# A transformer block with experts on one core: the kept rows and residuals of seven sequences get homes of their own and are loaded during the first group's blocks, the eighth's stay in SBUF

## The chip, the core and the metric

The kernel runs on one core of a Trainium2 chip. The metric is the time of one execution on the device in microseconds (us); lower is better. TensorE (PE) multiplies, VectorE (DVE), ScalarE (ACT) and GpSimd (POOL) do the elementwise work, SyncE (SP) issues most of the DMA transfers, POOL the indirect ones. Each engine, SP too, works through its own list of instructions in order, and waits on semaphores.

## The reference

Eight sequences of 512 tokens of width 256, all in fp32. `_L0_attn_ref` is causal attention with 16 heads and rotary positions; `_L0_ffn_ref` routes every token to 4 of 16 experts and adds a shared expert:

```python
x = L0_attn_x
x = x + _layernorm(_L0_attn_ref(_layernorm(x, axis=-1), ...), axis=-1)
x = x + _layernorm(_L0_ffn_ref(_layernorm(x, axis=-1), ...), axis=-1)
# inside _L0_ffn_ref, with cw the gates of the 4 chosen experts:
y = jnp.einsum('nei,ne,ehi->nh', act, cw, Wd)
shared = silu(xf @ Ws_g.T) * (xf @ Ws_u.T) @ Ws_d.T
return x + y + shared
```

So the last step of a sequence needs, per token, the four expert rows, the sum `z` of the shared expert's output and the normed input, and the residual `x1` from after the attention. `z` and `x1` (512 KB each for a sequence) are made early, in the attention part, and used at the very end. They are the "kept rows and residuals", and together the kept pair of a sequence (1 MB).

## The kernel before

**Stages.** The attention part runs over the sequences 0 to 7; at its end each sequence's normed rows are scattered by POOL into `sorted_rows` in DRAM, in the order of their experts. The sequences form two groups, 0 to 4 and 5 to 7 (`GROUPS`). The block part then takes the sorted rows 128 at a time. Two blocks are a pair: 48 pairs for group 0 and 32 for group 1, 80 in all (numbers 0 to 79 below). For each pair SP loads the rows (`BLD`, `load_block`, tile `xg`, four pairs of buffers), PE transposes (`BT1`, L1522), multiplies by gate and up weights (`BGU`, L1536), transposes (`BT2`, L1549) and multiplies down (`BDN`, L1557). In one iteration PE does `BT1` of pair j, `BGU` of j-1, `BT2` of j-2 and `BDN` of j-3. ACT copies the result of `BDN` into `ys` (three buffers), and POOL scatters it to `expert_rows` in DRAM. DVE's `block_notes` (L1038 to L1048) reads a pair's notes; it gives the places for the scatter and lets SP load the pair four further on.

**The end of a sequence.** When all pairs of a group are scattered, its sequences are summed in halves of 256 tokens. `CZ` (`load_residuals`, L637 and L638) loads a kept pair from DRAM into `zt` and `x1t`; `CL` (`load_sums`, L650) loads a half's expert rows, 1 MB, into `ykt`; `CA` sums them with `z`, `CS` takes statistics, `CN` makes the rows and stores them (`store_out`, L655). Group 0's sums run on DVE, beside group 1's blocks; group 1's run after all blocks, with PE doing the sums over experts (L1436). `ykt`, `zt` and `x1t` have two homes, by the parity of the sequence; sequence 7 has its own (`*_last`). So a kept pair can be loaded only when the sequence two before it has been stored.

**Order.** `make_plan` gives each step a time, sorts all steps, and every engine walks the same list. `sums(g)` lists the side steps of a group. Group 0's 45 steps are spread evenly over group 1's iterations 5 to 30; group 1's come after the last pair. The last sequence's work between attention and scatter is stretched (`late`) over the first 25 or so pairs of group 0. Also in SP's list: `PAD` (`pad_rows`, L610 and L611), 16 small writes of zeros for group 1's rows, between pairs 25 and 36, and `store_z`, `store_x1`, which write a sequence's `z` and `x1` tiles to DRAM. One DMA queue carries all of SP's transfers.

**Memory.** The block part lays `xg`, `ykt`, `zt`, `x1t` over the attention's tiles. The tiles `xr`, `pr`, `x1`, `z`, `a_hi`, `a_lo`, `silu`, `act` and `att` of the attention part are not used again once the last sequence is through.

Of the kernel before, what the change touches and what calls it, by code (L numbers as in the profile page):

```python
# [100 lines left out]
B_START = 3 * N_QUAD + 10  # L101


def sums(g):

    first, end = GROUPS[g]
    halves = [(s, h) for s in range(first, end) for h in range(2)]
    if end == B:

        steps = [("CZ", g, s) for s in range(first, end)] + [("CL", g, *half) for half in halves]  # L110
        for i, (s, h) in enumerate(halves):
            steps += [("CA", g, s, h), ("CS", g, s, h)]
            if i:
                steps.append(("CN", g, *halves[i - 1]))
        return steps + [("CN", g, *halves[-1])]
    steps = [("CZ", g, s) for s in range(first, min(first + 2, end))] + [("CL", g, *halves[0]), ("CL", g, *halves[1])]
    for i, (s, h) in enumerate(halves):
        if i + 2 < len(halves):
            steps.append(("CL", g, *halves[i + 2]))
        steps += [("CA", g, s, h), ("CS", g, s, h)]  # L120
        if i:
            steps.append(("CN", g, *halves[i - 1]))
        if h == 0 and first < s and s + 1 < end:
            steps.append(("CZ", g, s + 1))
# [14 lines left out]
def make_plan():  # L139
    timed = []  # L140

    def add(time, *step):
        timed.append((time, len(timed), step))

    per_seq = 3 * QUADS
    for s in range(B):
        for item in BEFORE + AFTER:
            add(per_seq * s + late(s, sooner(s, item[0], item[-1])) + FILL, item[0], s, *item[1:-1])
        for q in range(QUADS):
            add(per_seq * s + 3 * q - 4.7, "STL", QUADS * s + q)  # L150
    for g, (a, b) in enumerate(GROUPS):
        add(per_seq * (b - 1) + late(b - 1, 34.75) + FILL, "GE", g)
        add(per_seq * (b - 1) + late(b - 1, 38.1) + FILL, "GR", g)
        for e in range(E):
            add(per_seq * (b - 1) + late(b - 1, 35 + 0.42 * e) + FILL, "PAD", g, e)
        add(6 + 8 * g, "DUM", g)
    for Q in range(N_QUAD):
        for n in range(2 * UNITS):
            block, second = n // 2, n % 2
            add(3 * Q + block + (0.1, 0.3)[second], "S", Q, n // UNITS, n % UNITS)  # L160
            add(3 * Q + 7 + block + (0.0, 0.2)[second], "ST", Q, second, block)
        for m in range(UNITS):
# [12 lines left out]
    for g in range(len(GROUPS)):
        side = sums(g)
        begin = B_START + DUO0[g] + duos(g) + 5
        gap = (duos(g + 1) - 7) / len(side) if g + 1 < len(GROUPS) else 0.5
        for n, step in enumerate(side):
            add(begin + gap * n + 0.45, *step)  # L180
    return [step for _, _, step in sorted(timed)]
# [51 lines left out]
def block_kernel(nc, x, w_small, w_exp, rope, consts, out):  # L233
# [4 lines left out]
    with ctx:  # L238
# [42 lines left out]
        h_hi = place("h_hi", [P, KD, T], fp32r)  # L281
        h_lo = place("h_lo", [P, KD, T], fp32r)
        w_high = cursor[0]
        xr = place("xr", [P, 2, NT, XROW])
        pr = place("pr", [P, NT, D])
        x1 = place("x1", [P, NT, D])
        z = place("z", [P, NT, D])
        a_hi = place("a_hi", [P, 2, T], fp32r)
        a_lo = place("a_lo", [P, 2, T], fp32r)
        silu = place("silu", [P, 2, T])  # L290
        act = place("act", [P, 2, T])
        att = place("att", [P, NT, D])
        o_t = place("o_t", [P, T])
        mrow = place("mrow", [4 * NT, 2, P], fp32r)
# [76 lines left out]

        cursor[0] = w_low
        ykt_last = place("ykt_last", [P, NT, TOPK, D])
        zt_last = place("zt_last", [P, NT, D])
        x1t_last = place("x1t_last", [P, NT, D])
        assert cursor[0] <= w_high

        ident = kc[:, K_IDENT:K_IDENT + P]
        pcol = kc[:, K_PCOL:K_PCOL + 1]
# [100 lines left out]
        s_ys = sem("block_rows_out")  # L480
        s_ysc = [sem(f"block_scattered{i}") for i in range(NYS)]
        s_cl = [sem(f"parts_back{i}") for i in range(6)]
        s_cz = [sem(f"residuals_back{i}") for i in range(3)]
        s_cp = sem("results_summed")
        s_cs = sem("final_sums")
        s_cst = sem("final_stats")
        s_cv = sem("final_variance")
        s_cr = sem("final_rstd")
        s_cn = sem("final_rows")
        s_out = [sem(f"out_stored{i}") for i in range(3)]  # L490

        RELEASE = {
            "S": lambda st: (s_max, MAX_DONE[st[1:]]),
# [33 lines left out]

        def back(s):

            if s == B - 1:  # L530
                return ykt_last, zt_last, x1t_last
            return ykt[:, s % 2, :, :, :], zt[:, s % 2, :, :], x1t[:, s % 2, :, :]

        def sums_before(s, h):

# [8 lines left out]
        def _(sp):  # L544
# [85 lines left out]

            def load_residuals(s):
                _, z_home, x1_home = back(s)
                if turn(s) > 1:
                    sp.wait_ge(s_out[home(s)], 32 * (turn(s) - 1))
                sp.wait_ge(s_zst, 16 * (s + 1))
                sp.wait_ge(s_x1st, 16 * (s + 1))
                sp.dma_start(z_home[:, :, :], packed(z_dram[s])).then_inc(s_cz[home(s)], 16)  # L637
                sp.dma_start(x1_home[:, :, :], packed(x1_dram[s])).then_inc(s_cz[home(s)], 16)  # L638

            def load_sums(s, h):  # L640
                g = group_of(s)
# [10 lines left out]
            def store_out(s, h):  # L652
                sp.wait_ge(s_cn, N_OUT * (2 * s + h + 1))
                tiles = slice(NHALF * h, NHALF * h + NHALF)
                sp.dma_start(rows(out[s])[:, tiles, :], back(s)[1][:, tiles, :]).then_inc(s_out[home(s)], 16)  # L655

            load_x(0)
            sp.dma_start(stage[:, 0:C_O], w_small[:, 0:C_O]).then_inc(s_wq, 16)
# [4 lines left out]
            for st in PLAN:  # L663
# [8 lines left out]
                    maxima_rows(n)  # L672
                elif kind == "X1L":
                    load_x1(n)
                elif kind == "LNC":
                    store_x1(n)
                elif kind == "Z":
                    store_z(n)
                elif kind == "DUM":
                    zero_dummies(n)  # L680
# [4 lines left out]
                elif kind == "BLD":  # L685
                    load_block(n, st[2])
                elif kind == "CZ":
                    load_residuals(st[2])
                elif kind == "CL":
                    load_sums(st[2], st[3])  # L690
                elif kind == "CN":
                    store_out(st[2], st[3])
            for place_of in range(3):
                sp.wait_ge(s_out[place_of], 32 * max(turn(s) for s in range(B) if home(s) == place_of))


        @block.gpsimd
# [74 lines left out]
        def _(dve):  # L772
# [284 lines left out]
            def final_sums(s, h):  # L1057
# [1 line left out]
                y, z_home = back(s)[0][:, tiles, :, :], back(s)[1]  # L1059
                done = sums_before(s, h)  # L1060
                if s >= SHARED:
                    if h == 0:
                        dve.wait_ge(s_cz[home(s)], 32 * turn(s))
                    n = 2 * (s - SHARED) + h
                    dve.wait_ge(s_cp, n + 1)
                    total = ring[2][:, n % 2, :].rearrange("p (t d) -> p t d", t=NHALF)
# [3 lines left out]
                dve.tensor_tensor(y[:, :, 2, :], y[:, :, 2, :], y[:, :, 3, :], ALU.add).then_inc(s_cs, 1)  # L1070
                dve.tensor_tensor(y[:, :, 0, :], y[:, :, 0, :], y[:, :, 1, :], ALU.add).then_inc(s_cs, 1)
                if h == 0:
                    dve.wait_ge(s_cz[s % 2], 32 * (s // 2 + 1))
                dve.wait_ge(s_cs, done + 1)
                dve.tensor_tensor(y[:, :, 2, :], y[:, :, 2, :], zt[:, s % 2, tiles, :], ALU.add).then_inc(s_cs, 1)
                dve.wait_ge(s_cs, done + 3)
                dve.tensor_tensor(y[:, :, 0, :], y[:, :, 0, :], y[:, :, 2, :], ALU.add).then_inc(s_cs, 1)

# [561 lines left out]
```

## Time and profile before

| | |
|---|---|
| three runs | 980.75, 982.78, 987.75 us (median 982.78) |
| span of the profiled execution | 1048.8 us |
| PE busy | 852.6 us (81%) |
| VectorE busy | 652.3 us (62%) |
| ScalarE busy | 456.3 us (44%) |
| GpSimd busy | 426.7 us (41%) |
| DMA moved | 168.72 MB, mean 161 GB/s |
| SP's queue (q1) | 128.85 MB, 42.1% of 16 engines |
| POOL's queue (q0) | 38.55 MB, 9.9% |

Times in the trace count from the first instruction. A busy share is an average over stages with different limits: the attention part ends near 656 us, group 0's pairs leave from 674 to 885 us, group 1's from 888 to 1005 us, and the rest is the sums of sequences 5 to 7. The profiled execution is 66 us longer than the median of the runs, so a number of the trace is that of one, slower, execution.

### The profile page before, as it was taken

What the parts mean: (1) busy time and instruction counts of PE and PEld (TensorE: products, weight loads), DVE (VectorE), ACT (ScalarE), POOL (GpSimd) and SP (SyncE); (2) the same over time, 40 slices, a digit from 0 to 9 for tenths busy, and PEclk for the clock granted to TensorE, in tenths of its full rate; (3) what the DMA queues carried; (4) which work ended last, traced back from release to release, by engine and by line L of the source; (5) the groups of instructions that cost most, each with busy time, mean ns of one, the idle gap of its engine ahead of it and who ended that gap; (6) DMA issues with size and microseconds to landing.
All of it is one profiled execution on the core that took longest, in us unless ns stands there. A gap on an engine that the chain in (4) does not pass through costs nothing.

```text
span 1048.8 us, 20609 instructions
## 1 busy us (share of the span) xinstructions
PE 852.6 (81%) x6580; PEld 615.2 (59%) x6580; DVE 652.3 (62%) x1914; ACT 456.3 (44%) x763; POOL 426.7 (41%) x408
## 2 busy tenths in 40 slices
PE   4569798987987987987987877978977799989955
PEld 3436374664664663664654545757865588867722
DVE  5577658687687687687586674533642233687916
ACT  2115454544544544544543555425433355544410
POOL 3222113135335335335213234374565555664621
PEclk9759898997897897997987998889999999998978
DMA  4685726236336336336395212453545566997783
GB/s 161 147 222 144 216 64 163 75 98 174 98 99 173 99 99 173 98 81 172 98 322 159 85 47 92 144 167 93 166 150 161 161 178 164 383 314 281 247 339 128
DMA packets 89175, 168.72 MB, mean 161 GB/s; under 512 B 14704, under 2 KB 56688, under 8 KB 88816
## 3 DMA queue, kind: packets, MB, share of 16 engines
q1 hardware_dynamic: 75248, 128.85, 42.1%
q0 software_dynamic: 13824, 38.55, 9.9%
q8 instruction: 57, 0.93, 0.4%
q14 instruction: 46, 0.38, 0.1%
HBM read 90.15 MB, written 76.68 MB: 159 GB/s over the span
## 4 chain that ended last, share of the span: by engine, by line
PE 40%; DVE 23%; issue 11%; SPq 8%; DMA 6%; another core or an unknown queue 5%; ACT 4%; POOL 3%; DVEq 0%; ACTq 0%; POOLq 0%
DVE nmax L829 8%; PE ring L1536 6%; PE ring L1314 5%; PE ring L1316 4%; PE ring L1315 4%; PE ring L1392 3%; PE ring L1557 3%; PE ring L1358 2%; SPq L628 2%; PE ring L1383 2%; SPq L629 2%; DMA xg<-sorted_rows 2%; PE ring L1436 2%; PE ring L1522 2%
## 5 line engine op out<-in xcount | busy, mean ns | idle before, releaser
L1244 ACT ACTIVATE prob<-ring 128x1024 f32<-128x1024 f32 (+1 forms) x192 | 167.5, 881 | 215.5 <-PE ring L1383 196.5
L829 DVE TENSOR_REDUCE nmax<-ring 128x2 f32<-128x1024 f32 (+3 forms) x256 | 201.8, 819 | 73.3 <-PE ring L1365 43.6
L736 POOL DMA_INDIRECT expert_rows<-ys,dest x160 | 159.2, 995 | 127.0 <-ACT ys L1198 74.8
L728 POOL DMA_INDIRECT sorted_rows<-xr,idx_all x128 | 130.5, 1019 | 104.8 <-DVE xr L991 71.5
L1536 PE MATMUL ring<-we,xh 128*128 x640 | 160.3, 396 | 0.0
L1536 PEld LDWEIGHTS ring<-we,xh 128*128 128x128 f32 x640 | 121.6, 200 | 14.6
L1054 DVE SCALAR_TENSOR_TENSOR sl<-sl,got,ring 128x128 f32<-128x128 f32 x160 | 48.3, 343 | 109.8 <-ACT sl L1296 62.5
L1358 PE MATMUL ring<-k_st,q_st 48*128 48x512 f32 (+3 forms) x512 | 88.9, 387 | 26.0 <-issue 9.7
L1392 PE MATMUL ring<-prob,v_sb 128*32 128x512 f32 (+3 forms) x1024 | 106.3, 518 | 3.2 <-ACT prob L1244 3.2
L1377 PE MATMUL ring<-maskt_b,halves_b 64*128 64x128 bf16 (+2 forms) x768 | 58.4, 233 | 50.7 <-DVE nmax L829 23.5
L1377 PEld LDWEIGHTS ring<-maskt_b,halves_b 64*128 64x128 bf16 x768 | 22.8, 97 | 125.4 <-issue 56.7
L1383 PE MATMUL ring<-q_st,k_st 50*128 50x384 f32 (+3 forms) x512 | 94.1, 406 | 0.0
L1557 PE MATMUL ring<-we,ah 128*128 x320 | 86.4, 394 | 5.4 <-ACT ys L1198 4.1
L706 POOL TENSOR_TENSOR rot<-rot 128x512 f32<-128x512 f32 x14 | 17.9, 1276 | 172.7 <-DVE rot L810 172.7
L1522 PE MATMUL ring<-kc,xg 128*128 128x128 f32 x320 | 51.7, 286 | 28.2 <-DMA xg<-sorted_rows 22.3
L1358 PEld LDWEIGHTS ring<-k_st,q_st 48*128 48x128 f32 x512 | 51.7, 220 | 38.9 <-issue 11.8
L1296 ACT ACTIVATE sl<-ring 128x256 f32<-128x256 f32 x80 | 30.8, 385 | 92.4 <-PE ring L1536 56.9
L1198 ACT ACTIVATE ys<-ring 128x512 f32<-128x512 f32 x80 | 47.8, 598 | 43.6 <-PE ring L1557 20.3
L1198 ACT ACTIVATE xh<-ring 128x512 f32<-128x512 f32 x80 | 47.7, 596 | 40.6 <-PE ring L1522 23.9
L1522 PEld LDWEIGHTS ring<-kc,xg 128*128 128x128 f32 x320 | 40.5, 147 | 39.9 <-DMA xg<-sorted_rows 27.0
L1557 PEld LDWEIGHTS ring<-we,ah 128*128 128x128 f32 x320 | 56.3, 196 | 11.8 <-issue 6.9
L1365 PE MATMUL ring<-mask_b,halves_b 64*128 64x128 bf16 (+2 forms) x768 | 62.6, 247 | 0.0
(203 smaller groups left out, 1650.8 us busy)
## 6 DMA issues: line engine op xcount, KB each, us to landing
xg<-sorted_rows SPq DMA_DIRECT2D x160, 134.0 KB
parts<-part SPq DMA_DIRECT2D x32, 512.0 KB
ykt<-expert_rows SPq DMA_DIRECT2D x14, 1024.0 KB
k_st<-parts SPq DMA_DIRECT2D x64, 128.0 KB
q_st<-parts SPq DMA_DIRECT2D x64, 128.0 KB
we<-w_exp SPq DMA_DIRECT2D x1, 6144.0 KB
sorted_rows<-zeros SPq DMA_DIRECT2D x2, 2144.0 KB, 9.6
sorted_rows<-zeros SPq DMA_DIRECT2D x32, 134.0 KB
```

The costliest lines, as they stand in the source:

```text
L728: pool.indirect_dma_start(out=xs[group_of(s)], out_offset=bass.IndirectOffsetOnAxis(ap=idx_all[:, s, t, k:k + 1], axis=0), in_=xr[:, s % 2 ...
L736: pool.indirect_dma_start(out=yk, out_offset=bass.IndirectOffsetOnAxis(ap=dest[:, j % 8, b:b + 1], axis=0), in_=ys[:, j % NYS, b, :], in_o ...
L829: dve.tensor_reduce(nmax[:, Q % 2, :, pp, qb], slot[:, :, col:col + (qb + 1) * P], AX.X, ALU.max, negate=True).then_inc(s_max, 1)
L1198: act_e.activation(dst, src, ACT.Copy).then_inc(done, 1)
L1244: act_e.activation(prob[:, u % 2, 2 * half:2 * half + 2, 0:width], slot[:, :, 0:width], ACT.Exp, scale=SCALE).then_inc(s_exp, 1)
L1358: pe.matmul(slot[:, par, col:col + width], q_st[r, Q % NQ, pp, q0:q0 + P], k_st[r, Q % NQ, pp, 0:width], start=n == 0, stop=False, skip_gr ...
L1377: pe.matmul(blocks_of(slot[:, par, :], diagonal)[:, :, 0:64 * (h + 1)], halves_b[r, h, :], mask, start=h == 0, stop=False, skip_group_chec ...
L1383: last = pe.matmul(slot[:, par, col:col + width], k_st[r, Q % NQ, half, k0:k0 + P], q_st[r, Q % NQ, half, k0:T], start=False, stop=True, s ...
L1392: last = pe.matmul(O_BANK[32 * j:32 * j + 32, kb * P:T], v_sb[:, s % 2, kb, 4 * q + j, :], prob[:, u % 2, j, col:col + T - kb * P], start= ...
L1522: last = pe.transpose(X_BANK[:, b, k, :], xg[:, j % NXG, b, k * P:(k + 1) * P], ident)
L1536: last = pe.matmul(G_BANK[j % 2][:, b, :], xh[:, j % 2, b, k, :], we_cols[:, bass.ds(columns[j, b] + k * D, D)], start=(k == 0), stop=(k = ...
L1557: last = pe.matmul(Y_BANK[:, b, :], ah[:, j % 2, b, :], we_cols[:, bass.ds(columns.pop((j, b)) + KD * D, D)], start=True, stop=True)
```

## The change

- `sums` has no `CZ` steps any more. Seven `CZ` steps, in the order of sequences 0, 1, 2, 3, 5, 6, 4, stand at iterations 20, 23.5, ... 41 of group 0's blocks.
- Sequences 2 to 6 get homes of their own in the place of attention tiles that are dead by then: `kept_z2` to `kept_z6`, `kept_x2` to `kept_x6`. Sequences 0 and 1 keep `zt` and `x1t`. Sequence 7's pair isn't stored or loaded: the sums read the tiles `z` and `x1`.
- `load_residuals` waits for no output store now, but for all `z`, and for sequence 4 (whose home is `xr`) for all scatters of rows.
- The 40 side steps of group 0 are spread over the same iterations as the 45 before.

```diff
+KEPT_ORDER = [0, 1, 2, 3, 5, 6, 4]
+KEPT_START, KEPT_STEP = 20, 3.5
...
-        steps = [("CZ", g, s) for s in range(first, end)] + [("CL", g, *half) for half in halves]
+        steps = [("CL", g, *half) for half in halves]
...
-    steps = [("CZ", g, s) for s in range(first, min(first + 2, end))] + [("CL", g, *halves[0]), ("CL", g, *halves[1])]
+    steps = [("CL", g, *halves[0]), ("CL", g, *halves[1])]
...
-        if h == 0 and first < s and s + 1 < end:
-            steps.append(("CZ", g, s + 1))
...
+    for n, s in enumerate(KEPT_ORDER):
+        add(B_START + KEPT_START + KEPT_STEP * n + 0.45, "CZ", s)
...
-        zt_last = place("zt_last", [P, NT, D])
-        x1t_last = place("x1t_last", [P, NT, D])
+        kept_z6 = place("kept_z6", [P, NT, D])
+        kept_x6 = place("kept_x6", [P, NT, D])
         assert cursor[0] <= w_high
+
+
+        cursor[0] = xr_at
+        kept_z4 = place("kept_z4", [P, NT, D])
+        kept_x4 = place("kept_x4", [P, NT, D])
+        assert cursor[0] <= pr_at
+        kept_z5 = place("kept_z5", [P, NT, D], offset=pr_at)
+        kept_x5 = place("kept_x5", [P, NT, D], offset=att_at)
+        kept_z2 = place("kept_z2", [P, NT, D], offset=a_at)
+        kept_x2 = place("kept_x2", [P, NT, D], offset=a_at + NT * D * 4)
+        kept_z3 = place("kept_z3", [P, NT, D], offset=silu_at)
+        kept_x3 = place("kept_x3", [P, NT, D], offset=silu_at + NT * D * 4)
+        kept = [(zt[:, 0, :, :], x1t[:, 0, :, :]), (zt[:, 1, :, :], x1t[:, 1, :, :]), (kept_z2, kept_x2), (kept_z3, kept_x3),
+                (kept_z4, kept_x4), (kept_z5, kept_x5), (kept_z6, kept_x6), (z, x1)]
...
                 _, z_home, x1_home = back(s)
-                if turn(s) > 1:
-                    sp.wait_ge(s_out[home(s)], 32 * (turn(s) - 1))
                 sp.wait_ge(s_zst, 16 * (s + 1))
                 sp.wait_ge(s_x1st, 16 * (s + 1))
-                sp.dma_start(z_home[:, :, :], packed(z_dram[s])).then_inc(s_cz[home(s)], 16)
-                sp.dma_start(x1_home[:, :, :], packed(x1_dram[s])).then_inc(s_cz[home(s)], 16)
+                sp.wait_ge(s_z, NHALF * B)
+                if s == 4:
+                    for par in range(2):
+                        sp.wait_ge(s_sc[par], 256 * (B // 2))
+                sp.dma_start(z_home[:, :, :], packed(z_dram[s])).then_inc(s_cz[s], 16)
+                sp.dma_start(x1_home[:, :, :], packed(x1_dram[s])).then_inc(s_cz[s], 16)
...
-                elif kind == "LNC":
+                elif kind == "LNC" and n < B - 1:
                     store_x1(n)
-                elif kind == "Z":
+                elif kind == "Z" and n < B - 1:
                     store_z(n)
...
-                    if h == 0:
-                        dve.wait_ge(s_cz[home(s)], 32 * turn(s))
+                    if h == 0 and s < B - 1:
+                        dve.wait_ge(s_cz[s], 32)
...
-                dve.tensor_tensor(y[:, :, 2, :], y[:, :, 2, :], zt[:, s % 2, tiles, :], ALU.add).then_inc(s_cs, 1)
+                dve.tensor_tensor(y[:, :, 2, :], y[:, :, 2, :], z_home[:, tiles, :], ALU.add).then_inc(s_cs, 1)
```

How SP's list moves, at three places. First, SP in group 1, behind the `BLD` of pair 65 and ahead of that of pair 66, before:

```order
L629 DMA xg<-sorted_rows 128x268
L637 DMA zt<-z_rows 128x1024 [waits x1_stored,z_stored,out_stored0]
L638 DMA x1t<-x_rows 128x1024
L650 DMA ykt<-expert_rows 128x2x1024 [waits final_rows]
L628 TENSOR_LOAD tab [waits block_places,block_transposed]
```

and in the changed kernel at the load of the same expert rows (sequence 2, first half; L673 is the old L650, L649 and L650 the old L628 and L629):

```order
L678 DMA out<-zt 128x2x256 [waits final_rows]
L673 DMA ykt<-expert_rows 128x2x1024 [waits final_rows]
L649 TENSOR_LOAD tab [waits block_places,block_transposed]
L649 ISA x2
L650 ISA
L650 DMA xg<-sorted_rows 128x268
L649 TENSOR_LOAD tab
```

The two loads of the kept pair of sequence 2, with their wait for an output store, are gone from between `xg` and expert rows; an output store (L678) stands closer to them now. Second, SP beside the pads, before, at the ninth of the 16 pads (L610, L611) and the `BLD` of pair 31 behind it:

```order
L610 TENSOR_LOAD pad_idx [waits pad_places]
L610 ISA x2
L611 ISA
L611 DMA sorted_rows<-zeros 128x268
L628 TENSOR_LOAD tab [waits block_places,block_transposed]
L628 ISA x2
L629 ISA
L629 DMA xg<-sorted_rows 128x268
```

and in the changed kernel, at the same pad (L631, L632), with the kept pair of sequence 2 (`kept_z_151` is `kept_z2`, `kept_x_152` is `kept_x2`) between it and the `BLD`:

```order
L631 TENSOR_LOAD pad_idx [waits pad_places]
L631 ISA x2
L632 ISA
L632 DMA sorted_rows<-zeros 128x268
L660 DMA kept_z_151<-z_rows 128x1024 [waits z_ready,x1_stored,z_stored]
L661 DMA kept_x_152<-x_rows 128x1024
L649 TENSOR_LOAD tab [waits block_places,block_transposed]
L649 ISA x2
L650 ISA
L650 DMA xg<-sorted_rows 128x268
L649 TENSOR_LOAD tab
```

The rows are the same but for the two loads, which wait for all `z` and for the stores. Third, SP's end, before, from the last `xg` on:

```order
L629 DMA xg<-sorted_rows 128x268
L655 DMA out<-zt 128x2x256 [waits final_rows] x3
L637 DMA zt<-z_rows 128x1024 [waits x1_stored,z_stored,out_stored1]
L638 DMA x1t<-x_rows 128x1024
L637 DMA zt<-z_rows 128x1024 [waits x1_stored,z_stored,out_stored0]
L638 DMA x1t<-x_rows 128x1024
L637 DMA zt_last<-z_rows 128x1024 [waits x1_stored,z_stored]
L638 DMA x1t_last<-x_rows 128x1024
L650 DMA ykt<-expert_rows 128x2x1024 [waits block_scattered2,final_rows,block_scattered1,block_scattered0]
L650 DMA ykt<-expert_rows 128x2x1024 [waits final_rows] x3
L650 DMA ykt_last<-expert_rows 128x2x1024 x2
```

and in the changed kernel:

```order
L650 DMA xg<-sorted_rows 128x268
L678 DMA out<-kept_z_147 128x2x256 [waits final_rows] x2
L673 DMA ykt<-expert_rows 128x2x1024 [waits block_scattered2,final_rows,block_scattered1,block_scattered0]
L673 DMA ykt<-expert_rows 128x2x1024 [waits final_rows] x3
L673 DMA ykt_last<-expert_rows 128x2x1024 x2
```

The six loads between the last output stores of group 0 and the first expert rows of group 1 are gone.

## Rows read from the trace of the kernel before

**Rows 1.** Windows: engines' busy us, granted clock, DMA share, GB/s; last two stages

```profile
core 0 of [0], span 1048.8 us
...
757.00:840.00 83.00, 62.34 (x302) 49.87 (x301) 27.29 (x130) 29.83 (x68) 47.83 (x50) 0.94 0.50 158
...
888.00:1005.00 117.00, 103.33 (x530) 86.30 (x527) 83.46 (x291) 52.87 (x118) 70.51 (x73) 0.96 0.85 308
```

**Rows 2.** Timeline of ACT: `ys` copies of pairs 34, 54, 57, 62, 67, 72, 79

```profile
842.75 0.60 ACT L1198 ACTIVATE ys<-ring 128x512 f32<-128x512 f32 x1 [0.42 <-PE ring L1557]
...
907.75 0.60 ACT L1198 ACTIVATE ys<-ring 128x512 f32<-128x512 f32 x1 [0.43 <-issue]
...
920.21 0.60 ACT L1198 ACTIVATE ys<-ring 128x512 f32<-128x512 f32 x1 [0.52 <-PE ring L1557]
...
936.86 0.60 ACT L1198 ACTIVATE ys<-ring 128x512 f32<-128x512 f32 x1 [0.51 <-PE ring L1557]
...
960.90 0.60 ACT L1198 ACTIVATE ys<-ring 128x512 f32<-128x512 f32 x1 [0.81 <-issue]
...
980.99 0.60 ACT L1198 ACTIVATE ys<-ring 128x512 f32<-128x512 f32 x1 [0.42 <-issue]
...
1005.29 0.60 ACT L1198 ACTIVATE ys<-ring 128x512 f32<-128x512 f32 x1 [2.67 <-DMA expert_rows<-ys,dest]
```

**Rows 3.** Timeline of PE, group 1: start, us, and in brackets the wait before

```profile
941.04 1.12 PE L1522 MATMUL ring<-kc,xg 128*128 128x128 f32 x4 [4.22 <-DMA xg<-sorted_rows]
...
962.80 0.66 PE L1522 MATMUL ring<-kc,xg 128*128 128x128 f32 x4 [2.32 <-DMA xg<-sorted_rows]
...
983.00 0.66 PE L1522 MATMUL ring<-kc,xg 128*128 128x128 f32 x4 [2.05 <-DMA xg<-sorted_rows]
```

**Rows 4.** Chain of waits: start, us, what; loads from issue to landing

```profile
834.97 4.23 DMA xg<-sorted_rows
...
895.49 9.94 DMA ykt<-expert_rows
...
933.92 7.07 DMA xg<-sorted_rows
...
954.67 8.09 DMA xg<-sorted_rows
```

**Rows 5.** Timeline of SP's queue ahead of the first of the three waits

```profile
928.37 1.23 SPq L629 DMA_DIRECT2D xg<-sorted_rows  x2
929.90 0.20 SPq L637 DMA_DIRECT2D zt<-z_rows  x1
930.15 0.42 SPq L638 DMA_DIRECT2D x1t<-x_rows  x1
930.62 0.43 SPq L650 DMA_DIRECT2D ykt<-expert_rows  x1
```

**Rows 6.** DMA view of 892 to 1000 us: rate in 40 equal slices

```profile
GB/s 258 376 416 410 408 409 418 410 405 250 263 354 291 221 239 343 348 383 418 348 13 219 278 299 381 372 414 374 132 208 303 335 397 384 192 155 97 145 285 367
```

**Rows 7.** Tail: chain's scatters to landing, and POOL's next-to-last scatter in the timeline

```profile
995.42 6.52 DMA expert_rows<-ys,dest
...
1007.42 2.56 DMA expert_rows<-ys,dest
...
1006.16 0.96 POOL L736 DMA_INDIRECT expert_rows<-ys,dest  x1 [0.54 <-ACT ys L1198]
```

**Rows 8.** Pad stretch: chain on SP, SP's timeline after the pads, PE's waits 757 to 840

```profile
788.41 0.69 SPq L611
...
805.27 0.34 SPq L610
...
806.47 0.47 SPq L625
...
830.84 19.44 SPq L629 DMA_DIRECT2D xg<-sorted_rows  x15
...
PE ring L1522 <- DMA xg<-sorted_rows: 13.7, 8, 3.6
```

More of the change, by code:

```diff
@@ L283, in block_kernel @@
         w_high = cursor[0]
+        xr_at = cursor[0]
         xr = place("xr", [P, 2, NT, XROW])
+        pr_at = cursor[0]
         pr = place("pr", [P, NT, D])
@@ L287, in block_kernel @@
         z = place("z", [P, NT, D])
+        a_at = cursor[0]
         a_hi = place("a_hi", [P, 2, T], fp32r)
         a_lo = place("a_lo", [P, 2, T], fp32r)
+        silu_at = cursor[0]
         silu = place("silu", [P, 2, T])
         act = place("act", [P, 2, T])
+        att_at = cursor[0]
         att = place("att", [P, NT, D])
@@ L482, in block_kernel @@
         s_cl = [sem(f"parts_back{i}") for i in range(6)]
-        s_cz = [sem(f"residuals_back{i}") for i in range(3)]
+        s_cz = [sem(f"residuals_back{s}") for s in range(B - 1)]
         s_cp = sem("results_summed")
@@ L489, in block_kernel @@
         s_cn = sem("final_rows")
-        s_out = [sem(f"out_stored{i}") for i in range(3)]
+        s_out = sem("out_stored")
         RELEASE = {
@@ L528, in back @@
         def back(s):
-            if s == B - 1:
-                return ykt_last, zt_last, x1t_last
-            return ykt[:, s % 2, :, :, :], zt[:, s % 2, :, :], x1t[:, s % 2, :, :]
+            return ykt_last if s == B - 1 else ykt[:, s % 2, :, :, :], *kept[s]
         def sums_before(s, h):
@@ L654, in store_out @@
                 tiles = slice(NHALF * h, NHALF * h + NHALF)
-                sp.dma_start(rows(out[s])[:, tiles, :], back(s)[1][:, tiles, :]).then_inc(s_out[home(s)], 16)
+                sp.dma_start(rows(out[s])[:, tiles, :], back(s)[1][:, tiles, :]).then_inc(s_out, 16)
             load_x(0)
@@ L687, in _ @@
                 elif kind == "CZ":
-                    load_residuals(st[2])
+                    load_residuals(n)
                 elif kind == "CL":
@@ L692, in _ @@
                     store_out(st[2], st[3])
-            for place_of in range(3):
-                sp.wait_ge(s_out[place_of], 32 * max(turn(s) for s in range(B) if home(s) == place_of))
+            sp.wait_ge(s_out, 32 * B)
         @block.gpsimd
@@ L1072, in final_sums @@
                 if h == 0:
-                    dve.wait_ge(s_cz[s % 2], 32 * (s // 2 + 1))
+                    dve.wait_ge(s_cz[s], 32)
                 dve.wait_ge(s_cs, done + 1)
-                dve.tensor_tensor(y[:, :, 2, :], y[:, :, 2, :], zt[:, s % 2, tiles, :], ALU.add).then_inc(s_cs, 1)
+                dve.tensor_tensor(y[:, :, 2, :], y[:, :, 2, :], z_home[:, tiles, :], ALU.add).then_inc(s_cs, 1)
                 dve.wait_ge(s_cs, done + 3)
```

## The prediction

> **What bounds the kernel now.** I read the windows by stage first, then the times at which the blocks leave, then the chain of waits, and last the SP queue. The profiled execution spans 1048.8 us [rows 1], against a median of 982.78 us in the three runs. I make the sum in the profiled execution and carry its difference over to the median, and say below what the 66 us between them can do to it.
>
> The last of the four matmul steps of a pair of blocks ends in a `ys` copy. From pair 34 (842.75) to pair 54 (907.75) twenty pairs leave in 65.00 us [rows 2]: 3.25 us each, and PE is the bound there. From pair 54 to pair 79 (1005.29) 25 pairs take 97.54 us where 81.25 would do: 16.3 us are lost. This is the stretch in which group 0's sums run beside group 1's blocks, and the DMA engines are 0.85 busy in it, at 308 GB/s, against 0.50 and 158 in the stretch ahead [rows 1]. The 16.3 us split at the same rows: pairs 54 to 57 lose 12.46 - 9.75 = 2.71; 57 to 62 lose 16.65 - 16.25 = 0.40; 62 to 67 lose 24.04 - 16.25 = 7.79; 67 to 72 lose 20.09 - 16.25 = 3.84; 72 to 79 lose 24.30 - 22.75 = 1.55.
>
> The three large ones have one cause. PE waits for `xg` exactly three times, 4.22, 2.32 and 2.05 us [rows 3]. These transfers took 7.07 and 8.09 us to land (the first two are on the chain) where one in the quiet stretch took 4.23 [rows 4]. Ahead of each stands the same pattern on SP's queue, of which the first is shown: both tiles of a kept pair (`zt`, `x1t`, 1 MB), then 1 MB of expert rows, then the `xg` [rows 5]. The first loss, 54 to 57, has another form: the first load of expert rows stands behind two kept pairs (2 MB) and lands after 9.94 us [rows 4], and VectorE, which also makes the notes of each block, waits for it.
>
> **The change part by part.** (1) *Five kept pairs leave group 1's stretch* (5 MB). What one costs there: SP goes on from the end of the `xg` issue (928.37 + 1.23 = 929.60) to the issue of the expert rows (930.62), 1.02 us [rows 5]; and its bytes stand ahead of the `xg` in the queue. The DMA engines carry 408 to 418 GB/s when they are full [rows 6], so 1.05 MB takes 2.56 us. An `xg` behind it comes 3.6 us sooner. Against the waits of 2.32 and 2.05 that is enough, so 3.84 and 1.55 go; of 4.22 it leaves 0.6, and I keep 1.5 of the 7.79, for the gap and for a clock that may still dip: 6.3 saved. Of the 2.71 of the first burst I count half, 1.3: 2 MB fewer ahead of the first expert rows is 5.1 us, more than the wait, but VectorE still does two halves of sums between the notes of two pairs. Sum 13.0. Bounds: 16.3, if nothing is left; and 5.4 (3.84 + 1.55) if the first stall stays.
>
> The Trainium skill (DMA: Bandwidth & Descriptors, section "Where 436 GB/s comes from") puts the limit of HBM-to-SBUF traffic at about 358 GB/s for a core; the trace goes over that here. By the page's figure a kept pair would take 2.9 us, an estimate, and the first stall would shrink to about 0.3 us; the measured rate decides, and the sum stays.
>
> (2) *The tail.* Three kept pairs were issued while the last scatters ran; a scatter then took 6.52 us to land, and the last one, with the burst gone by, 2.56 [rows 7]. ACT's `ys` copies wait for those landings. But POOL has a backlog of scatters and sat idle only 0.54 us before its last two [rows 7], so no more than that comes off the end. I take 0.5 (bounds 0 and 2, if POOL starts its last run sooner). What follows, the loads of expert rows and PE's sums over them, reads nothing that the change touches.
>
> (3) *Spacing.* The 45 side steps of group 0 become 40 over the same 25 iterations, so a load has 1.9 iterations ahead of its sum (before 1.7). Nothing; the cover is VectorE's idle time.
>
> (4) *Two stores and a pair of loads of sequence 7 are gone.* The stores (1 MB) lie in group 0's stretch, which has half its DMA time free [rows 1]; nothing, at most the 1 us of two issues.
>
> (5) *Seven kept pairs enter group 0's blocks*, 14 DMAs on SP. None waits: all `z` were written before, the stores landed long ago, and the last scatters of rows are some ten iterations ahead of the pair of sequence 4, which alone needs them. Behind each stands a `BLD`, and PE waits for that. Three (sequences 5, 6, 4) fall where PE is full and SP stands up to four pairs ahead, 13 us, against 1.02 + 2.56: nothing. Four (0, 1, 2, 3) fall beside the 16 pad rows. There SP is itself near the bound: a pair's two `xg` take about 19.4 / 7.5 = 2.6 us, a pad 806.47 - 805.27 = 1.20 [rows 8]. Over the twelve pairs with 16 pads that is 12 x 2.6 + 16 x 1.2 = 50.4 us against PE's 39.0: 11.4 us over, and the lead of 13 us, less a landing of 4.23 [rows 4], covers 8.8. So before, some 2.6 us are already lost there and SP is the bound; what is added to SP counts in full. The pair of sequence 0 stands ahead of the pads, where SP has 3.25 - 2.6 = 0.65 us to spare with each pair and regains most of it; the other three stand among the pads, 3 x 1.02 = 3.1 us. The bytes add nothing lasting, as PE has room to catch up, but for the last: 2.56 at most. Take 3.0. Bounds: 0, if SP is quicker without the profiler, and 6.5.
>
> Sum: -13.0 - 0.5 + 3.0 = -10.5 us, so 1038.3 in this span's terms and 982.8 - 10.5 = 972.3 in the runs'.
>
> *The 66 us.* In this trace SP often advances one instruction in 0.7 us in the pad stretch (788.41, a register instruction, 0.69) [rows 8], and PE waits 13.7 us for `xg` there [rows 8]. Such steps are rare from 888 on, where the losses are tied to bytes. I hold the first for the profiler's own load, which the runs do not have, and the second for real. That is a choice, not something that the trace shows.
>
> **The rivals.** *A: as summed*, 972.3, own range 967 to 977. Chance 0.60. *B: more comes off*: nothing of 16.3 is left, POOL gains 2 and SP hides the moved loads: 982.8 - 18 = 965. For it: DMA demand falls from 0.85 x 117 = 99 us by 5 MB at 2.56, 13, to 86 us for 117 us. Chance 0.09. *C: the bursts of expert rows do the harm by themselves*: ten of 1 MB stay, each with an `xg` behind it, and the first stall (4.22) stays with its low clock; 5.4 + 0.5 - 3.0 = 2.9 comes off, 980. Against it: loads of expert rows without a kept pair ahead (two of three) made no wait of PE. Chance 0.22. *D: SP's queue becomes the bound, slower than before*: if the 0.7 us steps are real, a moved pair costs SP its five or so instructions at 0.7, 3.5 us, and a late `xg` 2.56 more; four of them 24 us, less 13.5: +10.7, 993.5. It decides from 3.4 us per moved pair on (4 x 3.4 = 13.6). For it: PE's 13.7 us of waits in this trace; against it: the runs are 66 us shorter than this trace, so they cannot hold all of it. Chance 0.09.
>
> That the change doesn't do what it says is no case: the order of SP's rows shows the loads gone from group 1.
>
> **How the numbers follow.** The range must leave out no more than 0.2: D (0.09) and a part of B and of C's far end; 964 to 982. One per cent is 9.8 us, to 972.95, and about what these runs (980.75 to 987.75) can tell from no change. A lies across that bound: 0.6 of it, 0.36, is faster, with B 0.45; the rest of A and C 0.46; D 0.09.
>
> **What would show it.** Right: no PE wait over 1 us for `xg` in group 1's pairs, pairs 54 to 79 in 84 us or so, DMA share there near 0.75, the first expert rows landing in 5 us, and the time from pair 20 to pair 34 longer by some 3 us. Wrong: a wait for `xg` behind expert rows alone (C), or SP late by more than 13 us in the pads, with PE waiting at each moved pair (D).

## The result, and the profile after

Over twenty runs each the changed kernel takes 978.94 us and the kernel before 985.43 us in the median: ratio 0.9941, 95% interval 0.9925 to 0.9958. A second comparison (label e13_after_again) gave 0.9944, 0.9921 to 0.9968. That is 5.8 us faster (4.1 to 7.4), where 10.5 was forecast. The sign is right, the size a bit over half.

The trace on record of the kernel before spans 66 us more than the runs take in the median, so two more were taken of it; they span 986.9 us (e0_before) and 984.8 us (e12_before_again). The second stands for the kernel before from here on. Its `ys` copies of pairs 20, 34, 54 and 79 (timeline of ACT; start, us, ..., wait before):

```profile
720.73 0.60 ACT L1198 ACTIVATE ys<-ring 128x512 f32<-128x512 f32 x1 [0.52 <-PE ring L1557]
...
775.10 0.60 ACT L1198 ACTIVATE ys<-ring 128x512 f32<-128x512 f32 x1 [0.57 <-PE ring L1557]
...
840.10 0.60 ACT L1198 ACTIVATE ys<-ring 128x512 f32<-128x512 f32 x1 [0.43 <-PE ring L1557]
...
941.27 0.60 ACT L1198 ACTIVATE ys<-ring 128x512 f32<-128x512 f32 x1 [3.04 <-DMA expert_rows<-ys,dest]
```

The same copies in the changed kernel, whose profiled execution spans 976.7 us:

```profile
720.59 0.60 ACT L1220 ACTIVATE ys<-ring 128x512 f32<-128x512 f32 x1 [0.51 <-PE ring L1579]
...
778.58 0.60 ACT L1220 ACTIVATE ys<-ring 128x512 f32<-128x512 f32 x1 [0.43 <-PE ring L1579]
...
843.58 0.60 ACT L1220 ACTIVATE ys<-ring 128x512 f32<-128x512 f32 x1 [0.43 <-PE ring L1579]
...
931.33 0.60 ACT L1220 ACTIVATE ys<-ring 128x512 f32<-128x512 f32 x1 [1.41 <-PE ring L1579]
```

Take 3.25 us per pair off each stretch, and what a stretch loses is left. (The last pairs, with fewer matmuls beside them, can leave less than 3.25 us apart, so a stretch that ends at pair 79 can lose less than nothing.) From the `ys` copies of each trace (us; the tail is from pair 79's copy to the end of the span):

| trace | pairs 20 to 34 | 34 to 54 | 54 to 79 | tail |
|---|---|---|---|---|
| before, on record | 25.7 | 0.0 | 16.3 | 43.5 |
| before, e0_before | 7.5 | 0.0 | 21.1 | 43.6 |
| before, e12_before_again | 8.9 | 0.0 | 19.9 | 43.5 |
| after | 12.5 | 0.0 | 6.5 | 45.4 |
| after, e13_after_again | 14.2 | 0.0 | 7.6 | 45.5 |

Between the means of the last two traces before and the two after: +5.2 us among the pads, -13.5 in group 1, +1.9 in the tail, together -6.4. That is the 5.8 us of the runs, within what they can tell. Two traces of a kernel differ by 1 to 2 us in a stretch, so the parts are no surer than that.

The cut at pair 79's copy divides things that belong together, and the 13.5 us have two halves. From pair 54 to 72 the loss went from 16.7 us to 10.0 (means of two traces each), from pair 72 to 79 from 3.9 to -2.9.

The three large waits of [rows 3] have these three in their place (timeline of PE after, group 1):

```profile
863.05 1.12 PE L1544 MATMUL ring<-kc,xg 128*128 128x128 f32 x4 [2.87 <-DMA xg<-sorted_rows]
...
888.70 0.66 PE L1544 MATMUL ring<-kc,xg 128*128 128x128 f32 x4 [1.28 <-DMA xg<-sorted_rows]
...
907.81 0.66 PE L1544 MATMUL ring<-kc,xg 128*128 128x128 f32 x4 [2.58 <-DMA xg<-sorted_rows]
```

and among the pads stand these three:

```profile
735.01 0.66 PE L1544 MATMUL ring<-kc,xg 128*128 128x128 f32 x4 [1.24 <-DMA xg<-sorted_rows]
...
748.79 0.66 PE L1544 MATMUL ring<-kc,xg 128*128 128x128 f32 x4 [3.70 <-DMA xg<-sorted_rows]
...
766.90 1.10 PE L1544 MATMUL ring<-kc,xg 128*128 128x128 f32 x4 [3.21 <-DMA xg<-sorted_rows]
```

Their sum and count against before (waits of PE, 720 to 780 us, e12_before_again and then after; us in total, times, longest):

```profile
PE ring L1522 <- DMA xg<-sorted_rows: 5.1, 5, 2.0
```

```profile
PE ring L1544 <- DMA xg<-sorted_rows: 8.1, 3, 3.7
```

So the waits themselves grew by 3.0 us and the stretch by 3.6 between these two traces. Between the other two, e0_before and e13_after_again, the waits went from 4.4 us to 8.7 and the stretch from 7.5 to 14.2. Behind a long wait PE is slow besides. The windows of the changed kernel behind two of the waits (from and to, length, busy us of PE, PEld, DVE, ACT and POOL, then granted clock, DMA share, GB/s) show a granted clock of 0.76:

```profile
749.00:756.00 7.00, 7.00 (x31) 5.83 (x30) 1.69 (x9) 2.45 (x5) 5.18 (x6) 0.76 0.76 242
767.00:774.00 7.00, 7.00 (x30) 5.98 (x31) 1.81 (x10) 2.34 (x5) 3.11 (x4) 0.76 0.75 232
```

One wait of 3.70 us made pair 28 leave 5.6 us late, one of 3.21 pair 32 by 5.1. So each cost 1.9 us more than its length. In the chain the eight matmuls behind the first took 2.87 us, against 1.73 at full clock:

```profile
743.92 4.82 DMA xg<-sorted_rows
748.75 0.04 issue
748.79 0.66 PE ring L1544 x4
749.45 2.87 PE ring L1558 x8
```

### The profile page after: what moved, and what is told of

Read it like the earlier page. It is cut to its first block, busy times and chain, and to the rows that moved or that the text cites. A ratio compares the mean times of both kernels' runs of the same rounds, so it can differ in the third digit from the quotient of the medians.

```text
span 976.7 us, 20603 instructions
## 1 busy us (share of the span) xinstructions
PE 819.3 (84%) x6580; PEld 601.5 (62%) x6580; DVE 651.2 (67%) x1914; ACT 453.5 (46%) x763; POOL 426.7 (44%) x408
## 4 chain that ended last, share of the span: by engine, by line
PE 49%; DVE 23%; issue 7%; DMA 6%; ACT 5%; SPq 5%; POOL 4%; DVEq 0%; ACTq 0%; POOLq 0%
PE ring L1558 10%; DVE nmax L851 7%; PE ring L1336 5%; PE ring L1338 4%; PE ring L1337 4%; PE ring L1579 4%; PE ring L1414 3%; DMA xg<-sorted_rows 3%; PE ring L1544 3%; PE ring L1380 3%; PE ring L1458 2%; PE ring L1350 2%; PE ring L1405 2%; POOL expert_rows L758 2%; PE ring L1399 2%
## 5 line engine op out<-in xcount | busy, mean ns | idle before, releaser
L1558 PE MATMUL ring<-we,xh 128*128 x640 | 156.4, 388 | 0.0
L1558 PEld LDWEIGHTS ring<-we,xh 128*128 128x128 f32 x640 | 119.2, 196 | 13.8
L1414 PE MATMUL ring<-prob,v_sb 128*32 128x512 f32 (+3 forms) x1024 | 100.0, 490 | 2.3 <-ACT prob L1266 1.4
L1380 PE MATMUL ring<-k_st,q_st 48*128 48x512 f32 (+3 forms) x512 | 86.1, 375 | 18.0 <-ACT prob L1266 9.1
L1405 PE MATMUL ring<-q_st,k_st 50*128 50x384 f32 (+3 forms) x512 | 90.1, 390 | 0.0
L1579 PE MATMUL ring<-we,ah 128*128 x320 | 83.2, 383 | 1.3 <-ACT ys L1220 1.3
L1380 PEld LDWEIGHTS ring<-k_st,q_st 48*128 48x128 f32 x512 | 49.5, 210 | 30.9 <-ACT prob L1266 15.5
L1387 PE MATMUL ring<-mask_b,halves_b 64*128 64x128 bf16 (+2 forms) x768 | 60.5, 239 | 0.0
```

The source lines that it names most:

```text
L1380: pe.matmul(slot[:, par, col:col + width], q_st[r, Q % NQ, pp, q0:q0 + P], k_st[r, Q % NQ, pp, 0:width], start=n == 0, stop=False, skip_gr ...
L1405: last = pe.matmul(slot[:, par, col:col + width], k_st[r, Q % NQ, half, k0:k0 + P], q_st[r, Q % NQ, half, k0:T], start=False, stop=True, s ...
L1414: last = pe.matmul(O_BANK[32 * j:32 * j + 32, kb * P:T], v_sb[:, s % 2, kb, 4 * q + j, :], prob[:, u % 2, j, col:col + T - kb * P], start= ...
L1558: last = pe.matmul(G_BANK[j % 2][:, b, :], xh[:, j % 2, b, k, :], we_cols[:, bass.ds(columns[j, b] + k * D, D)], start=(k == 0), stop=(k = ...
L1579: last = pe.matmul(Y_BANK[:, b, :], ah[:, j % 2, b, :], we_cols[:, bass.ds(columns.pop((j, b)) + KD * D, D)], start=True, stop=True)
```

## The experiments

Ratios are to the kernel before, run on the same chip, with their 95% intervals. Losses are counted as in the table above.

**The kernel before, twice more (no edit).**

> The kernel before, unchanged, for a second trace: the one on record spans 66 us more than the runs take. If the 0.7 us steps of SP in the pad stretch are the profiler's (my reading), they are gone here: pairs 20 to 34 take 45.5 us plus about 3, and pairs 54 to 79 still lose about 16 us, at three waits for xg behind kept pair and expert rows. The rival: part of the 16.3 us was the profiler's too, and this trace loses 10 us or less there; then the gain on group 1 was mis-sized, not the cost.

> The kernel before once more, for a third trace. Two traces lose 16.3 and 21.1 us between pairs 54 and 79, and the run with the tail alone, which has the same group 1, lost 16.8. If 17 is the usual figure, the change takes 10 us there (what was left after it is 6.5), and my 13.0 was too much; if 21 is, it takes 14 and the loss must be sought elsewhere.

The table has their numbers. The steps of 0.7 us on SP are gone from the pad stretch, and with them 17 to 18 of its 25.7 us. So they belong to that one execution and not to the kernel; that the profiler made them, as I had it, is not shown. Group 1 lost 21.1 and 19.9 us. Neither "10 or less" nor "17 is usual" held; the change takes 13.5 us there in the mean.

**The kept pairs behind the pads.**

```diff
-KEPT_START, KEPT_STEP = 20, 3.5
+KEPT_START, KEPT_STEP = 37, 1.5
```

> The changed kernel with the seven kept pairs issued from iteration 37 in steps of 1.5, behind the pads, where SP stands four pairs ahead. Theory 1 (the moved loads cost in the pad stretch: in the trace after, PE waits 1.24, 3.70 and 3.21 us for xg there, each with a slow clock behind it): pairs 20 to 34 take some 5 to 9 us less than in the changed kernel, and the ratio to before is 0.985 to 0.988. Theory 2 (the pads alone bind SP there, kept pairs or not): the pad stretch stays, ratio 0.994. Theory 3 (seven pairs within ten iterations are too dense): the waits move to pairs 37 to 47, ratio 0.994 or above.

0.9905 (0.9874 to 0.9937), 3.5 us better than the changed kernel in the ratio, though the two intervals overlap. The pads lose 8.3 us, as before the change (7.5 and 8.9), and pairs 34 to 54 lose 0.3, so seven kept pairs within ten iterations cost nothing where SP has its lead. Of theory 1 the place holds and the size is under (4 to 6 us less on the traces for 5 to 9, and 0.988 at most was expected); theory 3 falls. Theory 2 is right on one point: 8 us are lost among the pads with no kept pair there.

**The pads spread.**

```diff
-            add(per_seq * (b - 1) + late(b - 1, 35 + 0.42 * e) + FILL, "PAD", g, e)
+            add(per_seq * (b - 1) + late(b - 1, 35 + (0.42 if b < B else 0.8) * e) + FILL, "PAD", g, e)
```

> The changed kernel with the 16 pads of group 1 spread over about 20 iterations in place of 12; the kept pairs stay among them. Theory 1 and theory 2 both say that SP's work per pair binds: 2.6 + 0.8 x 1.2 + 0.29 x 1.0 = 3.9 us per pair still over PE's 3.25 in part, so a gain of 2 to 8 us over the changed kernel, ratio 0.986 to 0.992. If not SP's instructions but the bytes of the kept pairs make PE wait, the three waits stay where they are and the ratio is 0.994.

0.9920 (0.9893 to 0.9947). The loss of pairs 20 to 34 falls from 12.5 to 7.5 us and 3.6 come to pairs 34 to 54: SP has the same to do, and now over more pairs. The interval overlaps with that of the changed kernel, so a gain in time is not shown.

**What a moved pair costs: issues or bytes.** Each kept pair in eight transfers in place of two; DVE waits for the larger count.

```diff
-                sp.dma_start(z_home[:, :, :], packed(z_dram[s])).then_inc(s_cz[s], 16)
-                sp.dma_start(x1_home[:, :, :], packed(x1_dram[s])).then_inc(s_cz[s], 16)
+                for part_of in range(0, P, P // 4):
+                    r = slice(part_of, part_of + P // 4)
+                    sp.dma_start(z_home[r, :, :], packed(z_dram[s])[r]).then_inc(s_cz[s], 16)
+                    sp.dma_start(x1_home[r, :, :], packed(x1_dram[s])[r]).then_inc(s_cz[s], 16)
```

> The changed kernel with each kept pair loaded in eight transfers of 128 KB in place of two of 512 KB: the same bytes, 6 more issues on SP for each pair at about 0.45 us. If what a moved pair costs among the pads is SP's time (issue), four pairs add 4 x 2.7 = 10.8 us to pairs 20 to 34 over the changed kernel's 12.5 us of loss, and the ratio is 1.003 to 1.007. If it is the bytes ahead of the next xg, the stretch stays near 12.5 us and the ratio at 0.994 to 0.996.

1.0050 (1.0021 to 1.0079), and pairs 20 to 34 lose 21.5 us, 9.0 more than in the first trace of the changed kernel and 7.3 more than in the second, with the same bytes; 10.8 was expected. Pairs 34 to 54 lose another 2.5. That points to SP's time, and in the pad stretch of the changed kernel SP waits for others 0.4 us in all. One piece takes SP 0.41 to 0.43 us, and the next starts 0.46 us after it (timeline of SP's queue in this run):

```profile
727.44 0.41 SPq L662 DMA_DIRECT2D zt<-z_rows  x1
727.89 0.42 SPq L663 DMA_DIRECT2D x1t<-x_rows  x1
728.36 0.42 SPq L662 DMA_DIRECT2D zt<-z_rows  x1
728.82 0.43 SPq L663 DMA_DIRECT2D x1t<-x_rows  x1
```

This run tells that added issues are paid for in large part; it does not say that the bytes cost nothing, nor whether eight pieces of 32 partitions land as soon as two of 128.

**Either part alone.** First the end alone: sequence 7 stays in SBUF, 5 and 6 load behind the pads, and 0 to 4 in group 1 as before.

```diff
-KEPT_ORDER = [0, 1, 2, 3, 5, 6, 4]
-KEPT_START, KEPT_STEP = 20, 3.5
+KEPT_ORDER = [5, 6]
+KEPT_START, KEPT_STEP = 37, 3.5
...
-    steps = [("CL", g, *halves[0]), ("CL", g, *halves[1])]
+    steps = [("CZ", s) for s in range(first, first + 2)] + [("CL", g, *halves[0]), ("CL", g, *halves[1])]
...
+        if h == 0 and first < s and s + 1 < end:
+            steps.append(("CZ", s + 1))
```

> One part alone: sequence 7's pair stays in SBUF and those of 5 and 6 are loaded behind the pads, while the pairs of 0 to 4 are loaded in group 1's stretch as before. My sum gives this part 0.5 us (bounds 0 and 2): ratio 0.999, 0.998 at the least. The rival, that the bursts at the end hold up the last scatters and with them PE's last pairs: 3 to 4 us, ratio 0.996 to 0.997.

0.9990 (0.9968 to 1.0012): no difference that these runs can tell, as the sum had it. Its trace loses 16.8 us in pairs 54 to 79 and has a tail of 45.3: what pairs 72 to 79 gain (1.6 us lost in place of 3.5 and 4.2) the tail gives back (45.3 in place of 43.5 and 43.6).

Then group 1 alone: 0 to 4 behind the pads, 5, 6 and 7 stored and loaded at the end.

```diff
-KEPT_ORDER = [0, 1, 2, 3, 5, 6, 4]
-KEPT_START, KEPT_STEP = 20, 3.5
+KEPT_ORDER = [0, 1, 2, 3, 4]
+KEPT_START, KEPT_STEP = 37, 1.5
...
-        steps = [("CL", g, *half) for half in halves]
+        steps = [("CZ", s) for s in range(first, end)] + [("CL", g, *half) for half in halves]
...
-                elif kind == "LNC" and n < B - 1:
+                elif kind == "LNC":
...
-                elif kind == "Z" and n < B - 1:
+                elif kind == "Z":
```

> The other part alone: the kept pairs of sequences 0 to 4 are loaded behind the pads and are gone from group 1's stretch, while those of 5, 6 and 7 are stored and loaded at the end as before. If the gain is group 1's (theory 1), this has nearly all that the kernel with all seven behind the pads has (0.9905): 0.990 to 0.993, and pairs 54 to 79 lose 5 to 8 us instead of 16 to 21. If the two parts need one another, since a faster group 1 only runs into the burst at the end, the ratio is 0.995 or above, and pairs 76 to 79 leave late.

0.9897 (0.9864 to 0.9929), with 7.1 us lost in pairs 54 to 79 and a tail of 43.6. With all seven behind the pads it was 0.9905 (e1), so the whole of the gain is group 1's. The treatment of 5, 6 and 7 adds nothing that can be told.

**The output stores held back.** SP walks past a store of group 0 and issues it up to three loads of blocks later. On the changed kernel (e10), with pads spread and kept pairs from iteration 44 on (`KEPT_START, KEPT_STEP = 44, 1.2`) without it (e8) and with it (e9):

```diff
+            held = []
...
+                if held and (kind == "BLD" or st[0] == "CN" or (kind == "CL" and st[2] >= SHARED)):
+                    held[0][0] -= 1
+                    while held and (held[0][0] <= 0 or kind == "CL"):
+                        store_out(*held.pop(0)[1])
...
+                elif kind == "CN" and st[2] < SHARED:
+                    held.append([3, (st[2], st[3])])
```

> Both remedies: the 16 pads spread over 20 iterations and the seven kept pairs behind them, at iterations 44 to 52, the last quiet ones. SP's work over pairs 25 to 53 is then 28 x 2.6 + 16 x 1.2 + 7 x 1.02 = 99 us against PE's 91 and its lead of 9: if SP's time is what binds (theory 1), the waits for xg of 20 to 34 shrink from 8.3 to 2 to 4 us and none comes after: ratio 0.984 to 0.988. If the pad stretch has another bound (the scatters of sequence 7, which run there too), ratio 0.990.

> The kernel with both remedies and group 0's output stores held back on SP for up to three loads of blocks. In the trace after, what is left of group 1's loss (6.5 us, 4.5 of it at pair 60) comes behind a store that SP reaches 4.3 us before VectorE has its rows, with the next xg queued behind it. If that wait is the cause, pair 60's loss goes and the stretch loses 1 to 3 us: ratio 0.980 to 0.985. If the four loads of expert rows ahead are the cause, by their bytes, nothing changes against the kernel without this.

> The changed kernel with only group 0's output stores held back on SP for up to three loads of blocks. If the loss left at pair 60 comes from the store that SP waits in, it goes here too: 3 to 5 us less in pairs 54 to 79, ratio 0.989 to 0.991. If it needs the remedies of the pad stretch as well, or stems from the expert rows ahead, the ratio stays at 0.994.

| | ratio | 95% interval | loss 20 to 34 | 34 to 54 | 54 to 79 |
|---|---|---|---|---|---|
| e8, both remedies | 0.9888 | 0.9852 to 0.9924 | 3.9 | 3.4 | 4.2 |
| e9, with stores held | 0.9845 | 0.9821 to 0.9870 | 4.0 | 4.6 | 1.3 |
| e10, stores held alone | 0.9916 | 0.9899 to 0.9932 | 13.0 | 0.0 | 1.0 |

In the changed kernel pair 60 alone loses 4.5 us, and the second trace has 4.3 at pair 62. Here SP's queue ahead of it (timeline after):

```profile
842.70 3.77 SPq L650 DMA_DIRECT2D xg<-sorted_rows  x4
849.99 0.41 SPq L678 DMA_DIRECT2D out<-zt  x1
851.21 1.67 SPq L650 DMA_DIRECT2D xg<-sorted_rows  x2
852.92 0.43 SPq L673 DMA_DIRECT2D ykt<-expert_rows  x1
854.18 4.25 SPq L650 DMA_DIRECT2D xg<-sorted_rows  x4
```

SP is free at 846.5 and stands before the store until 850; all that follows is late, and the `xg` issued at 855.55, with 1 MB of expert rows ahead of it, lands after 7.46 us. With the stores held, and the loads of expert rows as they were, PE's waits for `xg` in group 1 go from 6.7 us to 0.7 (waits of PE, 843 to 932 us, after and then e10_after_stores_held):

```profile
PE ring L1544 <- DMA xg<-sorted_rows: 6.7, 3, 2.9
```

```profile
PE ring L1551 <- DMA xg<-sorted_rows: 0.7, 1, 0.7
```

So what is left in group 1 is the wait in SP's list, and the expert rows' bytes only matter behind it. The traces show this, the runs only lean that way. The stretch gains 5.5 us on the trace (3 to 5 expected), and the ratio is 2.8 us better than e13's, just above the 0.991 expected; the two intervals overlap. So do those of e8 and e9, which differ by the held stores alone. The pads keep their 13 us, so the two faults are apart. e8 gave less than expected; its interval reaches what was expected. e9 came out as expected, at the upper end.

The store is no new obstacle. SP stands before the same stores in the kernel before too, 27.8 us in all against 21.4; in both, a part of that comes behind the last load of blocks (waits of SP, 835 to 945 us in e0_before, then 835 to 925 us after):

```profile
SPq L655 <- DVE zt L1101: 17.6, 6, 7.1
SPq L655 <- DVE zt L1098: 10.2, 1, 10.2
```

```profile
SPq L678 <- DVE kept_z L1123: 9.0, 4, 3.3
SPq L678 <- DVE zt L1123: 7.8, 2, 4.3
SPq L678 <- DVE kept_z L1120: 4.6, 1, 4.6
```

No run holds the stores back in the kernel before. How much of its loss would go by that alone, with the kept pairs where they were, is open.

**The changed kernel once more.**

> The changed kernel once more, for a second trace and beside its variants on one chip. Its pads should again lose 12 to 13 us between pairs 20 and 34 (5 over the kernel before), pairs 54 to 79 6 to 7 us with 4.5 at pair 60, and the ratio be 0.993 to 0.996.

0.9944, as expected. The pads lost 14.2 us and pairs 54 to 79 7.6, a little more, and the largest loss stood at pair 62, not 60.

**The best version.** As e9, with the pairs of sequences 0 and 1 ahead of the pads and the other five from iteration 45 on.

```diff
-KEPT_START, KEPT_STEP = 20, 3.5
+KEPT_START, KEPT_STEP = 45, 1.6
...
-    for n, s in enumerate(KEPT_ORDER):
+    for s, at in ((0, 10), (1, 15)):
+        add(B_START + at + 0.45, "CZ", s)
+    for n, s in enumerate(KEPT_ORDER[2:]):
         add(B_START + KEPT_START + KEPT_STEP * n + 0.45, "CZ", s)
...
-                sp.wait_ge(s_z, NHALF * B)
+                if s > 1:
+                    sp.wait_ge(s_z, NHALF * B)
```

> All remedies (pads spread, stores held, kept pairs behind the pads), and the pairs of sequences 0 and 1, whose homes are free from the start of the blocks, loaded ahead of the pads at iterations 10 and 15, beside the last sequence's work, where PE is slower than SP. The traces with kept pairs at 44 to 52 lose 3.4 to 4.6 us between pairs 34 and 54, since SP has no lead left; with two fewer there it should be 1 to 2: ratio 0.981 to 0.984. If SP has no lead to spare at 10 and 15 either, 0.985.

0.9813 (0.9800 to 0.9826), 967.16 us, as expected. Pairs 34 to 54 lose 0.9 us in place of 4.6, but pairs 0 to 20 lose 21.5 where the other traces, but for the slow one on record, have 16.8 to 18.5, so part of it was paid there. All of group 1 now waits 1.7 us for `xg` or less (waits of PE, 843 to 932 us):

```profile
PE ring L1554 <- DMA xg<-sorted_rows: 1.7, 3, 0.9
```

## Why the prediction was off

**What bounds the kernel: right in the main, but half of the cause.** The loads of kept pairs in group 1 do harm there: group 1 alone gives the whole gain. The waits for `xg` at pairs 63, 68 and 73 are gone; but three others stand in the changed kernel, at pairs 60, 67 and 72. My "one cause" left out the output store that SP stands before ahead of the same loads. Ahead of the second of the three waits, in the trace on record (timeline of SP's queue), SP is free at 943.60 and issues nothing until the store at 948.03; ahead of the third it is 3.8 us:

```profile
939.67 3.93 SPq L629 DMA_DIRECT2D xg<-sorted_rows  x4
948.03 0.40 SPq L655 DMA_DIRECT2D out<-zt  x1
```

**Term 1, 13.0 us off group 1: 13.5 on the traces, and that is luck.** I took 13.0 of 16.3 us and left 3.3. The later traces lose 20.5 us before the change and keep 7.0 after it: both ends were off by about 4 us, and the difference hides it. Nor did it come where I had it. From pair 54 to 72 I had forecast 11.4 us less and 6.7 went; from pair 72 to 79 I had forecast 1.6 and 6.8 went, 2.2 of it also with the part at the end alone (e4). The first burst's loss went wholly (pairs 54 to 57 lose nothing; I had counted half). The step that failed is "An `xg` behind it comes 3.6 us sooner" and that this is enough, so that only 1.5 us of the stalls stay: once the kept pair is gone, the next `xg` still comes late, since SP stands before a store ahead of it. Pair 60 or 62 loses 4.5 or 4.3 us by that, and pairs 67 and 72 between 1.4 and 3.9 when they lose. With the stores held the stretch keeps 1.0 us (e10). The Trainium skill's limit of about 358 GB/s (DMA: Bandwidth & Descriptors, "Where 436 GB/s comes from") played no part; in the tail the windows show 421 to 424 GB/s.

**Term 2, 0.5 us off the tail: behind pair 79 the sign is wrong, 1.9 us more.** It rested on POOL's idle time before its last two scatters. I took the gap as something to gain and did not ask what a faster PE runs into. In the changed kernel pairs 77, 78 and 79 leave 2.8, 2.0 and 2.0 us apart, and POOL needs 2.53 for a pair. Its timeline has no gap left over the last four scatters, the last of them 3.2 us after pair 79's copy (before: 2.1):

```profile
930.72 0.96 POOL L758 DMA_INDIRECT expert_rows<-ys,dest  x1 [0.30 <-issue]
931.99 0.96 POOL L758 DMA_INDIRECT expert_rows<-ys,dest  x1 [0.30 <-issue]
933.25 0.96 POOL L758 DMA_INDIRECT expert_rows<-ys,dest  x1 [0.30 <-issue]
934.52 0.96 POOL L758 DMA_INDIRECT expert_rows<-ys,dest  x1 [0.30 <-issue]
```

That is 1.1 us. The other 0.8 is PE: it takes 23.9 us for the sums at the end, before 23.1. The windows over the first ten microseconds of these sums, before (e12_before_again) and after:

```profile
950.71:955.71 5.00, 5.00 (x7) 2.16 (x8) 0.00 (x0) 0.00 (x0) 0.00 (x0) 0.56 1.03 421
955.71:960.71 5.00, 5.00 (x13) 2.15 (x12) 2.52 (x7) 0.00 (x0) 0.72 (x1) 1.00 1.03 424
```

```profile
941.79:946.79 5.00, 5.00 (x6) 2.19 (x7) 0.00 (x0) 0.00 (x0) 0.00 (x0) 0.50 1.03 421
946.79:951.79 5.00, 5.00 (x12) 2.08 (x11) 1.88 (x6) 0.00 (x0) 0.72 (x1) 0.89 1.03 422
```

The granted clock is at its lower level, 1.2 GHz, for longer after the change; ahead of it PE had sat idle for about as long (10.5 us, before 11.1). Why it rises later was not tried. The 1.9 us are no loss by themselves: the part at the end alone (e4) gave 0.9990, so what it takes off pairs 72 to 79 and what it adds behind them cancel, and as the worth of that part the 0.5 us hold within what the runs can tell.

**Term 5, 3.0 us among the pads: the mechanism right, the size under: 5.2 (3.6 to 6.7, by which traces are compared).** The pairs of sequences 1, 2 and 3 each have their wait, and SP's time is most of what is paid (e7). The waits grew by 3.0 and 4.3 us. What the sum left out is that a long wait costs PE more than its length, by the slow clock behind it: 5.6 for 3.70 and 5.1 for 3.21. Each of the two traces before has one such wait in the stretch (2.00 us, which cost 3.9, and 3.12, which cost 4.9), each of the two after has two. I had the price of such a wait in hand: the first stall of group 1 lost 7.79 us over a wait of 4.22.

**The sum.** -13.5 + 1.9 + 5.2 = -6.4 where -13.0 - 0.5 + 3.0 = -10.5 stood. Behind pair 54, where terms 1 and 2 are best taken together, 11.6 us went and 13.5 were forecast; the pads cost 2.2 us more than forecast. That makes the 4.1 us. I set SP's 0.7 us steps aside, and two traces without them bear that out: rival D fell with them. Rival C gave 980, near the result, but by a mechanism (the expert rows' bytes by themselves) that e10 refutes. Of the signs named beforehand: no `xg` wait over 1 us in group 1: wrong, three; pairs 54 to 79 in 84 us: 87.75; DMA share near 0.75 there: 0.73; the first expert rows landing in 5 us: 6.0 (before 9.9); pairs 20 to 34 longer by 3 us: 3.6 to 6.7.

## What to carry to other kernels

A transfer moved out of a crowded stretch is paid in the issuing engine's time where it lands. Count that engine's work per iteration there, its lead, and what it spends before each wait; a load is free only where the engine is ahead by more than the issue and the landing. A store that waits for a late result should not stand in a queue ahead of loads that others need soon. And a gain is worth only what the slowest engine behind it can follow: ask for each microsecond off the front which engine is next at the end. Before a late load is put down to the one ahead of it, read every wait of the issuing engine back from there, and read the loss in more than one trace before taking a part off it.

## What the runs showed of the hardware

- A wait of PE of 2.00 us cost 3.9 us, waits of 3.21, 3.37 and 3.70 cost 5.1, 5.3 and 5.6: 1.9 us over their length each, while waits of 1.24 and 1.59 cost 0.25 and 0.4 over theirs. Behind the longer ones the granted clock over the next seven microseconds is 0.76, and eight matmuls take 2.87 us for 1.73. At two waits of 3.48 and 3.70 us it is 0.58, and they cost 3.1 us over their length. Other waits over 2 us in these traces cost 0.4 to 2.7 over theirs.
- SP takes mostly 0.36 to 0.47 us to issue a 2D transfer, whether it moves 128 KB or 512 KB, and 1.1 to 1.2 us for one whose address it loads from a table first; in this kernel those are some 2.3 to 2.4 us for each pair of blocks, not far from PE's 3.25.
- One profiled execution held stretches in which SP advances one instruction in 0.7 us that two later ones of the same kernel do not have: the same 14 pairs lost 25.7 us in the one trace and 7.5 and 8.9 in the others.
